# A two-layer windowed-attention network around a delta-rule memory: transposes grouped, the last step of the gated product moved to VectorE, one subtraction put behind the statistics

## The reference

```python
x = x + 0.5 * ffn(layernorm(x))        # DEPTH = 2 layers
x = x + ttt(layernorm(x))              # linear memory, step by step
x = x + 0.5 * ffn(layernorm(x))

def layer(x):                          # HEADS 8, DIM_HEAD 64, WINDOW 128, HID 682
    h = shift_token(x)                 # right half of the columns one row later
    q, k, v = split(h @ wqkv)          # 256 x 1536
    q, k = l2norm(q) * qs, l2norm(k) * ksc
    q, k = rotary_xpos(q, k)
    # window i attends to itself and the window before, masked, softmax(8 q k)
    o = local_attention(q, k, v)
    x = x + o @ wo
    h = shift_token(x)
    h = (h - mean(h)) / sqrt(var(h) + 1e-5) * lg + lb
    a, g = split(h @ w1 + b1)
    return x + (a * gelu(g)) @ w2 + b2
```

## Time and profile before

| | |
|---|---|
| time, median of 3 runs | 2761.85 us (2761.56 to 2762.11) |
| the profiled execution | 2763.2 us |
| its span, first to last instruction | 2761.4 us |
| granted TensorE clock, mean | 0.992 |
| PE busy | 2679.1 us (97%), 23280 products |
| PEld busy | 2313.4 us (84%) |
| DVE busy | 2205.2 us (80%) |
| ACT busy | 1753.8 us (64%) |
| POOL busy | 1580.6 us (57%) |
| chain that ended last | PE 69%, DVE 15%, ACT 7%, issue 5%, POOL 3%, DMA 1% |

### The profile page before, as it was taken

One profiled execution on the slowest core, in us unless ns is written; L12 is line 12 of the kernel. 1 busy time (PEld: TensorE's weight loads), 2 busy tenths in 40 slices (PEclk: granted clock), 3 DMA queues, 4 the chain that ended last, 5 costly groups with the idle time before them and its releaser, 6 DMA issues.

```text
span 2761.4 us, 66715 instructions
## 1 busy us (share of the span) xinstructions
PE 2679.1 (97%) x23280; PEld 2313.4 (84%) x23280; DVE 2205.2 (80%) x6398; ACT 1753.8 (64%) x4748; POOL 1580.6 (57%) x1758
## 2 busy tenths in 40 slices
PE   7999999999999999998999999999999999999999
PEld 6888888888888888887766888888888888888887
DVE  7888888887878887776655888877778888888886
ACT  4666666666666666665454667666666666666665
POOL 4666666656565666654212566655656566656654
PEclk8999999999999999999999999999999999999999
DMA  3121011003000000005100000000003000000000
GB/s 116 32 78 64 20 51 55 21 19 112 13 2 2 2 2 24 2 4 191 33 17 32 2 2 2 2 2 2 2 2 112 33 2 17 17 17 17 17 17 24
DMA packets 75899, 81.33 MB, mean 29 GB/s; under 512 B 37552, under 2 KB 61872, under 8 KB 74416
## 3 DMA queue, kind: packets, MB, share of 16 engines
q1 hardware_dynamic: 73888, 75.61, 8.4%
q10 hardware_dynamic: 1680, 1.46, 0.2%
HBM read 49.53 MB, written 26.74 MB: 28 GB/s over the span
## 4 chain that ended last, share of the span: by engine, by line
PE 69%; DVE 15%; ACT 7%; issue 5%; POOL 3%; DMA 1%; SPq 0%; DVEq 0%; ACTq 0%; POOLq 0%
PE bank L1018 11%; PE bank L1020 10%; PE bank L1019 10%; PE bank L1219 8%; PE bank L1108 6%; PE bank L1094 6%; PE bank L1078 4%; PE bank L1054 3%; ACT pr L767 3%; PE bank L1363 2%; DVE h L1609 2%; DVE t L1523 2%; DVE t L1520 2%; PE bank L1139 2%; POOL pr L605 1%
## 5 line engine op out<-in xcount | busy, mean ns | idle before, releaser
L605 POOL TENSOR_TENSOR pr<-pr,rden 128x512 f32<-128x512 f32 (+1 forms) x512 | 470.8, 941 | 464.0 <-DVE rden L1557 460.0
L767 ACT ACTIVATE pr<-pr,nb 128x256 f32<-128x256 f32 (+1 forms) x1024 | 478.8, 469 | 325.4 <-DVE nb L1548 325.3
L1548 DVE CUSTOM_DVE_ANT_0 pr<-bank,maskb,r 128x256 f32<-128x256 f32 (+1 forms) x1024 | 401.5, 446 | 15.2 <-PE bank L1078 3.5
L1018 PE MATMUL bank<-h2T,w 128*128 128x256 f32 x1408 | 405.8, 288 | 3.9
L1019 PE MATMUL bank<-h2T,w 128*128 128x256 f32 x1408 | 394.9, 280 | 0.0
L1020 PE MATMUL bank<-h2T,w 128*128 128x256 f32 x1408 | 394.7, 280 | 0.0
L632 POOL TENSOR_TENSOR uTl<-t,uTh 128x256 fp32r<-128x256 f32 x320 | 240.6, 752 | 267.4 <-ACT uTh L842 265.4
L1623 DVE SCALAR_TENSOR_TENSOR t<-bank,b,t 128x256 f32<-128x256 f32 (+1 forms) x384 | 181.9, 480 | 173.8 <-ACT t L827 103.1
L1018 PE MATMUL bank<-wqkv,hT 128*128 128x512 f32 x768 | 305.0, 397 | 8.7 <-DVE nb L1548 6.4
L1019 PE MATMUL bank<-wqkv,hT 128*128 128x512 f32 x768 | 304.7, 397 | 0.0
L1020 PE MATMUL bank<-wqkv,hT 128*128 128x512 f32 x768 | 301.7, 393 | 0.0
(11 more groups left out here) (229 smaller groups left out, 7042.1 us busy)
## 6 DMA issues: line engine op xcount, KB each, us to landing
wqkv<-wqkv_split SPq DMA_DIRECT2D x18, 512.0 KB, 6.4
w<-w_split SPq DMA_DIRECT2D x3, 2816.0 KB, 9.9
Y<-in_x SPq DMA_DIRECT2D x8, 512.0 KB, 8.2
stt<-stt SPq DMA_DIRECT2D x256, 3.0 KB
out<-Y SPq DMA_DIRECT2D x8, 512.0 KB, 3.5
h<-out SPq DMA_DIRECT2D x7, 512.0 KB, 3.9
out<-h SPq DMA_DIRECT2D x7, 512.0 KB, 2.9
wqkv_split<-wqkv SPq DMA_DIRECT2D x1, 3072.0 KB, 11.7
```

The source lines that it names most:

```text
L605: e.tensor_tensor(pr[:, 2 * j:2 * j + 2, 0:wide], pr[:, 2 * j:2 * j + 2, 0:wide], rden[:, 2 * j:2 * j + 2].unsqueeze(2).to_broadcast([P, 2 ...
L767: last = e.activation(pr[:, hd, 0:wide], pr[:, hd, 0:wide], ACT.Exp, bias=nb[:, hd:hd + 1], scale=-1.0, accum_out=den[:, hd:hd + 1])
L1018: e.matmul(out, left[0], right[0], start=first, stop=False)
L1548: m = e.tensor_tensor_reduce(pr[:, hd, 0:wide], bank[j][:, g * 256:g * 256 + wide], far, r[:, t, 1, place(hd):place(hd) + 1], FAR, ALU.add ...
```

## The change

It has six parts, all of them in the order of work; no arithmetic is added or dropped.

1. TensorE: the four blocks of `PT` are issued together, then `fill(1)`, then the four of `PV`. `PT_BANK` becomes 4, 5, 3, 2: the last block goes to bank 2 and waits until ScalarE has copied v out of it.
2. TensorE: `fill(2)` goes ahead of `A0`, so `A0`, k's and q's `A2` are one block of transposes.
3. The last high part and the last low part of a batch's gated product, the high part so far on ScalarE and the low part on GpSimd, become `U_last` on VectorE, behind the second and the third reciprocal of the next batch's tile 0.
4. Tile 0: ScalarE squares k ahead of the last two exponentials; VectorE sums k's squares ahead of the fourth reciprocal (`squares`, split off `A1`); GpSimd adds the bias (`XB`) behind `A1` and not ahead of the normalizations.
5. Tile 3: VectorE makes q's low part behind the residual and the statistics (`A2` is split into `A2_k` and `A2_q`).
6. Tile 3's moves: ScalarE issues a move of 127 rows, SyncE the single row; before it was the other way round.

```diff
-PT_BANK = (4, 5, 3, 4)
+PT_BANK = (4, 5, 3, 2)
...
-        def move_first_row(e, t, q):
-            e.dma_start(stt[P - 1:P, t, 12:18], stt[0:1, t, 0:6]).then_inc(q, 16)
+        def move_first_halves(e, t, q):
+            e.dma_start(stt[0:P - 1, t + 1, 12:18], stt[1:P, t, 0:6]).then_inc(q, 16)
...
                 e.dma_start(stt[1:P, t, 6:12], stt[0:P - 1, t + 1, 18:24]).then_inc(q, 16)
-                e.dma_start(stt[0:P - 1, t + 1, 12:18], stt[1:P, t, 0:6]).then_inc(q, 16)
-                if 0 < t < 3:
-                    move_first_row(e, t, q)
+                if t < 3:
+                    move_first_halves(e, t, q)
+                if t:
+                    e.dma_start(stt[P - 1:P, t, 12:18], stt[0:1, t, 0:6]).then_inc(q, 16)
...
# GpSimd, sequence
-                    if prev:
+                    if prev and t:
                         XB(*prev, t)
                     for j in range(4):
                         NP(L, b, t, j)
                     if ahead:
                         A1(*ahead)
+                    if prev and t == 0:
+                        XB(*prev, t)
...
-                    for i in range(1, MT):
+                    for i in range(1, MT - half):
                         U_lo(L, b, half, i)
...
# ScalarE, sequence
-                    for j in range(4):
+                    for j in range(3):
                         S(L, b, t, j)
+                    if t == 0:
+                        A1_k(*ahead)
+                    S(L, b, t, 3)
+                    if ahead and t:
+                        A1_k(*ahead)
                     if ahead:
-                        A1(*ahead)
+                        A1_qv(*ahead)
...
                 e.wait_ge(st_done, at(st_done, idx(L, b, 3) + 1))
-                move_first_row(e, 3, st_moved[1])
+                move_first_halves(e, 3, st_moved[1])
...
                 table(ACT.Exp)
-                U_hi(L, b, 2 * MT - 1)
...
# TensorE, PT
                 if j == 2:
                     e.wait_ge(nb_done, at(nb_done, 4 * n + 4))
+                elif j == 3:
+                    if t < NT - 1 or more:
+                        e.wait_ge(v_sb, at(v_sb, n + 2))
                 else:
-                    e.wait_ge(pt_sb, at(pt_sb, 4 * n + (0, -2, 0, 1)[j]))
+                    e.wait_ge(pt_sb, at(pt_sb, 4 * n - 3 + j))
...
# VectorE
+            def U_last(L, b, part):
+
+                f = 8 * L + b
+                if part == 0:
+                    e.wait_ge(u_done, at(u_done, 12 * f + 12))
+                    e.wait_ge(u_hi, at(u_hi, 12 * f + 11))
+                    e.tensor_copy(uTh[:, 1, JOBS[-1], :], ut[:, 1, :]).then_inc(u_hi, 1)
+                else:
+                    e.wait_ge(u_hi, at(u_hi, 12 * f + 12))
+                    e.wait_ge(u_lo, at(u_lo, 10 * f + 9))
+                    e.tensor_tensor(uTl[:, 1, JOBS[-1], :], ut[:, 1, :], uTh[:, 1, JOBS[-1], :], ALU.subtract).then_inc(u_lo, 1)
...
                     for j in range(1, 4):
+                        if t == 0 and j == 3:
+                            squares(idx(*ahead), 0)
                         R(L, b, t, j)
+                        if t == 0 and prev and j < 3:
+                            U_last(*prev, j - 1)
...
                     if ahead:
-                        A2(*ahead)
+                        A2_k(*ahead)
+                    if ahead and t < 3:
+                        A2_q(*ahead)
                     WO(L, b, t)
                     halves(L, b, t)
+                    if ahead and t == 3:
+                        A2_q(*ahead)
```

50 lines of the change are left out of this document (30 added, 20 removed).

## The result

The changed kernel took 2716.7 us (median of 4 runs, 2715.3 to 2721.4) beside 2762.0 us for the kernel before on the same chip (4 runs): a ratio of 0.984, with an interval of 0.982 to 0.986. The prediction was 2723 us, with 2702 to 2746 as its range. The direction was right and the size too cautious by 6 us. The profiled execution spans 2715.3 us where it spanned 2761.4, so 46.1 us are to be accounted for and the sum had 38.7. Behind this small difference two terms of the sum are too small (tile 0, and tiles 1 and 2) and one is too large (parts 5 and 6), and the experiments found two things in the change that the prediction had not priced: the place of two waits and the completion of the moves.

What follows compares the result with a forecast made beforehand. TensorE's own stream and its few waits were taken to bound the kernel. Terms 18.0 (tile 0) + 15.5 (tiles 1 and 2) + 5.2 (statistics) = 38.7 us, giving 2723 us, range 2702 to 2746.

Steps and rivals of the forecast that it cites:

- Part 1 (0.25 a tile): Tiles 1 and 2: merged transposes and value products take 3.84 instead of 4.11 us; 0.25 over 62 tiles, 15.5 us.
- the transition to second products: Tiles 1 and 2, TensorE: second product straight behind a value product, never seen in the trace; 0.27 us taken as 0.25.
- Part 2 (zero): k's and q's transposes together on TensorE: no costly transition removed, zero gain, 0.05 either way.
- Parts 3 and 4, tile 0 (0.75 in 24 batches): Tile 0: VectorE's rotation 0.95 us earlier, output product 0.75 earlier; 24 batches, 18.0 us.
- The first layer (zero): Tile 0 of first layer's batches 1 to 6: entry statistics fill the idle time; zero gain, 0 to 0.35 us slower each.
- Rotation stays where it was: First layer's tile 0, VectorE: two new steps push the fourth reciprocal 1.3 us back, leaving the rotation's start unchanged.
- Tile 3 (wait 0.55, hidden): Tile 3: TensorE waits about 0.55 us for the fourth normalization, hidden behind busy VectorE; 0.1 of loss, absorbed later.
- Part 5 (0.18): Behind tile 3: q's lower part moved makes statistics and the chain behind them 0.18 us earlier; 29 batches, 5.2 us.
- part 6 (zero): Tile 3's two 127-row moves issued from SyncE and ScalarE: the moving engine sets the rate, so zero gain.
- The queue: Rival, tile 3's moves: the queue sets their pace, so split issue saves 21.8 us more, 2701 us; chance 0.10.
- VectorE blocked in tile 0: Rival: VectorE's two new steps each wait about 0.9 us for a GpSimd normalization; slower, 2767 us; chance 0.07.
- It starts first: Tile 0: VectorE issues its new step right behind the reciprocal releasing GpSimd, so it gets the shared port pair first.

Runs made afterwards that it cites:

- experiment 7: Changed kernel with the second product's pieces again between k's and q's transposes: 2717.6 us (kernel before 2762.9; ratio 0.9836).
- Experiment 5: Kernel before with only VectorE's two waits for the gated product's parts moved behind k's sum of squares in tile 0: 2757.6 us (before 2762.9; ratio 0.9981).
- experiment 9: Changed kernel with k's early squares undone, ScalarE squaring behind all eight exponentials and VectorE summing behind the fourth reciprocal: 2730.2 us (before 2762.8; ratio 0.9883).
- experiment 8: Changed kernel with the gated product's last high part back on ScalarE, last low part on GpSimd: 2729.8 us (before 2762.8; ratio 0.9877).
- experiment 10: Changed kernel with SyncE issuing both 127-row moves, plus six second products later, k squared earlier, half its rotation before the fourth reciprocal: 2738.6 us (before 2762.9).

## Why the prediction held, point by point

- **Part 1 (0.25 a tile).** Mechanism right, term too small. The blocks save 0.33 (3.79 against 4.12), and all of it arrives, 0.34 a tile. The 0.02 put down for the transition to second products doesn't exist, and the block lengths were 0.05 too long. Against that, tile 2 of the first layer's six batches gained nothing (15.17 to 15.13), where the sum had counted it. In all it is 18.9 us in place of 15.5.
- **Part 2 (zero).** Right: experiment 7.
- **Parts 3 and 4, tile 0 (0.75 in 24 batches).** VectorE's times were met to 0.07: sum at 5.23 (5.29 predicted), rotation 6.11 (6.14), free for o 10.56 (10.49). What was mis-sized is the price of two of TensorE's blocks: three second products 0.54, not 0.64, sixteen value products 1.02, not 1.15. With them ScalarE's copy of o seemed to be the last; in fact VectorE is. So 0.95, not 0.75. And the right figure for the sum hid a cause: the prediction let it follow the squares by 0.05 where the trace of before had 0.20, and did not say why. Experiment 5 shows that this is the place of two waits, 0.16 a batch. So some 4 us of this term were met by an omission, which is luck.
- **The first layer (zero).** Wrong: 0.5 us gained in each of the six. "Rotation stays where it was" failed. VectorE's two steps took 0.20 and 0.32 from start to start, 0.52 together and not 0.8, and its idle time before k's sum is gone. The rotation starts 6.63 us into the tile; it was 7.11. The early squares are not the reason: in experiment 9, without them, the rotation starts at 6.63 as well, since by then the earlier exponentials have brought the squares forward. In experiment 8, without VectorE's two steps, it starts at 6.49. Two rows of the changed kernel's layer 0, batch 3 (its tile 0 starts at 268.20):

```profile
274.76 0.15 DVE L1575 RECIPROCAL rden<-den 128x2 f32<-128x2 f32 x1
274.83 0.67 DVE L1528 TENSOR_TENSOR t<-bank,rot 128x512 f32<-128x512 f32 x1
```

- **Tile 3 (wait 0.55, hidden).** Right: a wait of 0.44, the tile 0.02 longer, and 0.03 shorter without it.
- **Part 5 (0.18), part 6 (zero).** Both mis-sized, in opposite directions. The statistics are 0.23 earlier, and since VectorE's later steps are held for 0.12 less, 0.38 arrives at the end. Part 6 takes back 0.31 of it, 0.19 in the completion of the moves and the 0.12 again. The argument for part 6 looked at the rate of the packets alone, and the rate stayed; the cost is in the 0.51 us between the last packet and the moments. By the sentence of the Trainium skill that the prediction draws on, two issuers save issue time only; by the measurement, which decides, two were 8 us slower here than one. Together the two parts give 0.07 in place of 0.18.
- **The rivals.** The queue does not set the pace: the rate stayed at 4 GB/s, and with it 2701 fell. VectorE blocked in tile 0: its two new steps took 0.29 and 0.42 us, not 0.9, and GpSimd's third normalization 0.73 in place of 0.61. "It starts first" was right here. In experiment 10, two of GpSimd's steps were the ones held.

What stays open: why two engines' issue makes the moments come 0.18 later behind the last packet. In the changed kernel SyncE's second issue takes 1.33 us where it took 0.60 (medians 1.30 and 0.83); its queue is the last to finish, but which of its two moves completes last isn't told apart. The clock's share of experiment 8's 5 us is not measured. GpSimd's later bias, the rest of part 4, was never undone by itself; that the three other shares of tile 0 add up to 0.95 leaves it little, and does not show it.

## What to carry to other kernels

When a step is moved off a chain, read all three engines' chains in that stretch before moving the next: here VectorE, GpSimd and TensorE were within 0.3 us of each other, and a move that gave VectorE 0.18 cost GpSimd 1.4. Look at where waits stand, not only at where work stands; put those that are met long ago behind the first instruction that really waits, if that one does not need them. A wait that grows to the longest of the list (from 6 to 20 us for the normalization) may cost next to nothing, and a change of issuing engine that is meant to be free should be measured by itself.

## What the runs showed of the hardware

- Two met waits ahead of an open one cost VectorE 0.16 us from the release to its start (0.20 against 0.04).
- Two moves of 127 rows issued from two engines at once are no faster than from one: packets of 24 bytes, 254 in 1.5 us, both ways; the packets of the two queues take turns. VectorE, which waits for them, starts 0.51 us behind the last packet, not 0.33.
- VectorE's normalization step of 0.34 us took 0.76 to 0.88 beside GpSimd's 0.74; GpSimd's guard of 0.24 us took 0.76 and its product of 1.04 took 1.43 beside VectorE's addition `t<-t` of 0.69. The hold goes both ways, and moving a chain by 0.2 us changes who is held.
